# Attention block on one core: Yh's weights set over zeros so that the last product runs as 128x128 matmuls, four tiles of x, x loaded in quarters, small norms by one-tensor operations

## The reference, cut to what matters

```python
qkv = einsum('bcxy,oc->boxy', group_norm(x), w_qkv);  q, k, v = split(qkv)
k = softmax(k, axis=-1)
context = einsum('ndm,nem->nde', k, v)
content_out = einsum('nde,ndm->nem', context, q)
Sx = einsum('ndxy,xid->nixy', q4, Px)            # Px: relative row table
Yh = einsum('nixy,neiy->nexy', Sx, v4)
Yh = batch_norm(Yh)                               # one mean and variance per e, over all images and heads
Sy = einsum('ndxy,yid->nixy', q4, Py)            # Py: relative column table
rel_pos_out = einsum('nixy,nexi->nexy', Sy, Yh)
x + einsum('bcxy,oc->boxy', content_out + rel_pos_out, w_out) + b_out
```

## Time and profile before

| | |
|---|---|
| median of 3 runs | 3025.26 us (3024.06 to 3027.86) |
| the profiled execution | 3016.12 us, span 3014.0 us |
| mean granted clock of PE | 0.953 of full speed |
| busy: PE, PEld, DVE, ACT, POOL | 2656.9, 2127.2, 1875.2, 1544.1, 1248.7 us |
| matmuls | 61044 |
| bytes moved by the transfers | 383.62 MB, 127 GB/s on average |

### The profile page before, as it was taken

One profiled execution on the slowest core, in us unless ns is written; L12 is line 12 of the kernel. 1 busy time (PEld: TensorE's weight loads), 2 busy tenths in 40 slices (PEclk: granted clock), 3 DMA queues, 4 the chain that ended last, 5 costly groups with the idle time before them and its releaser, 6 DMA issues. The chain is left out here.

```text
span 3014.0 us, 131462 instructions
## 1 busy us (share of the span) xinstructions
PE 2656.9 (88%) x61044; PEld 2127.2 (71%) x61044; DVE 1875.2 (62%) x2986; ACT 1544.1 (51%) x2884; POOL 1248.7 (41%) x557
## 2 busy tenths in 40 slices
PE   2999999999998998999989986887979888888889
PEld 1788787787787877878778775666666666666665
DVE  5567667676676676676675556655555555555553
ACT  1565565655656656566565553444443444344443
POOL 2244334424325335244253336544444444454641
PEclk9999999999999999999999997899999999999999
DMA  3233434425325235234235337767666766666663
GB/s 143 60 85 115 100 74 128 102 59 149 81 66 162 61 77 153 60 90 139 70 98 121 95 94 159 176 173 173 176 171 174 173 173 171 168 175 182 178 179 106
DMA packets 433042, 383.62 MB, mean 127 GB/s; under 512 B 297840, under 2 KB 364656, under 8 KB 430448
## 3 DMA queue, kind: packets, MB, share of 16 engines
q1 hardware_dynamic: 414064, 341.66, 44.1%
q10 hardware_dynamic: 18432, 33.56, 3.1%
HBM read 206.31 MB, written 168.82 MB: 124 GB/s over the span
## 5 line engine op out<-in xcount | busy, mean ns | idle before, releaser
L787 POOL TENSOR_TENSOR k_f<-k_f,negmax 128x1024 f32<-128x1024 f32 x128 | 303.4, 2399 | 851.7 <-DVE negmax L752 851.7
L430 PE MATMUL bank<-w_hi,x_hi 128*128 128x256 f16 x2048 | 576.6, 282 | 39.0 <-POOL x_lo L771 23.4
L430 PE MATMUL bank<-w_lo,x_hi 128*128 128x256 f16 x2048 | 570.7, 279 | 2.5 <-issue 2.5
L430 PE MATMUL bank<-w_hi,x_lo 128*128 128x256 f16 x2048 | 569.9, 278 | 0.3 <-issue 0.3
L1241 POOL TENSOR_TENSOR x_f<-x_f,y_norm_by 128x1024 f32<-128x1024 f32 x127 | 273.3, 2152 | 552.5 <-DMA x_f<-y_scratch 550.2
L697 DVE TENSOR_TENSOR v_lo<-bank,v_hi 128x256 f16<-128x256 f32 x512 | 213.5, 420 | 261.7 <-ACT v_hi L565 260.6
L564 ACT ACTIVATE k_f<-bank 128x256 f32<-128x256 f32 x512 | 199.5, 390 | 315.3 <-PE bank L430 314.3
L1205 DVE TENSOR_TENSOR o_lo<-bank,o_hi 128x512 f16<-128x512 f32 x256 | 167.0, 684 | 279.6 <-ACT o_hi L1117 279.2
L1015 PE MATMUL bank<-q,rc_both 128*64 128x64 f16 x4096 | 276.2, 245 | 64.6 <-DMA q<-q_scratch 32.7
L1117 ACT ACTIVATE o_hi<-bank 128x512 f16<-128x512 f32 x256 | 142.1, 594 | 370.7 <-PE bank L1046 370.7
L430 PEld LDWEIGHTS bank<-w_hi,x_hi 128*128 128x128 f16 x2048 | 297.5, 145 | 47.4 <-issue 23.5
(11 more groups left out here) (146 smaller groups left out, 8293.3 us busy)
## 6 DMA issues: line engine op xcount, KB each, us to landing
y_scratch<-yst SPq DMA_DIRECT2D x256, 256.0 KB, 3.8
x_f<-y_scratch SPq DMA_DIRECT2D x256, 256.0 KB, 5.3
q<-q_scratch SPq DMA_DIRECT2D x256, 256.0 KB, 4.7
x_f<-x SPq DMA_DIRECT2D x16, 2048.0 KB, 11.3
q_scratch<-q_hi SPq DMA_DIRECT2D x128, 256.0 KB, 3.4
q_scratch<-q_lo SPq DMA_DIRECT2D x128, 256.0 KB, 4.1
x_res<-x SPq DMA_DIRECT2D x128, 256.0 KB, 6.9
out<-x_res ACTq DMA_DIRECT2D x128, 256.0 KB, 3.3
```

Source lines behind the costliest of these rows:

```text
L430: mm = pe.matmul(outs, lhs[a], rhs[m], start=first and n == 0, stop=last and n == 2, **kw)
L787: pool.tensor_tensor(kk, kk, negmax[:, :].unsqueeze(1).to_broadcast([P, 8, P]), ALU.add).then_inc(shifted, 1)
```

## The change

Half two, the product: `yb_hi` and `yb_lo` get one more dimension of 2 before the channel, [128, 32, 2, 64, 2]. Partitions 0 to 63 (the first head) fill index 0 and hold zeros at index 1; partitions 64 to 127 hold zeros at index 0. So the weights of one x and both heads are one 128x128 matrix with two 64x64 blocks and zeros elsewhere, and one 128x128 matmul of 64 columns takes the place of two 64x64 ones. The zeros are set once by four memsets on DVE. ACT and DVE fill the two blocks by one operation on 64 partitions each, in place of one on 128, and the semaphores count 8 pieces a head. Both content sets stand ahead of the products, and each bank of the pair signals when it is filled.

The tiles: twice the size of `yb` is made up for by `XS` = 4 slots of `x_res`, and by `st` and `y_norm_by`, which now lie in other tiles. The loads into the slots are moved: tiles 0 to 3 at the last two pairs of head 2, 4 to 11 at the second and fourth pair of head 3, 12 to 15 at the second pair of head 0.

The loads of q: by head of the pair and in halves of x. One (half, head) part is two transfers of the same bytes as before but twice the length of a piece (2 KB). They are issued after the second and third ro pair (one part each) and after the fourth (two parts).

Half one: the small operations of the two norms that read two tensors from SBUF become `tensor_scalar` with per-partition scalars, one for each channel block where needed. The next image is loaded in quarters of a channel block, with a semaphore for each block, spread over heads 0 and 1 of the turn.

```diff
-                for c in range(CC):
-                    sp.dma_start(x_f[:, c, :], x_chunks[0, c]).then_inc(x_in, 16)
+                def load_x(index, c, quarter):
+                    s = slice(quarter * XC, quarter * XC + XC)
+                    sp.dma_start(x_f[:, c, s], x_chunks[index, c][:, s]).then_inc(x_in[c], 16)
...
+                            if order is not final_turn and hp < CC and (hp, quarter) != (0, 0):
+                                load_x(b + 1, hp, quarter)
+                        next_x(0)
                         store_ys(0, 1)
                         if hp < HP - 1:
                             store_q(0)
+                        next_x(1)
                         store_ys(2, 3)
...
-                    dve.scalar_tensor_tensor(ymv[:, 1:2], ymv[:, 0:1], ymv[:, 0:1], ymv[:, 1:2],
-                                             ALU.mult, ALU.add).then_inc(y_stats, 1)
+                    dve.tensor_scalar(ymv[:, 1:2], ymv[:, 0:1], ymv[:, 0:1], ymv[:, 1:2],
+                                      ALU.mult, ALU.add).then_inc(y_stats, 1)
                     dve.wait_ge(y_stats, n + 3)
-                    dve.tensor_tensor(acc[:, :], acc[:, :], ymv[:, :], ALU.add).then_inc(y_stats, 1)
+                    for k in range(2):
+                        o = dve.tensor_scalar(acc[:, k:k + 1], acc[:, k:k + 1], ymv[:, k:k + 1], None, ALU.add)
+                    o.then_inc(y_stats, 1)
...
-                    dve.tensor_tensor(rstd[:, :], gs[:, :, 0], gs[:, :, 0], ALU.mult).then_inc(bn_done, 1)
-                    dve.wait_ge(bn_done, base + 2)
-                    dve.tensor_tensor(rstd[:, :], gs[:, :, 1], rstd[:, :], ALU.subtract).then_inc(bn_done, 1)
+                    for c in range(CC):
+                        dve.tensor_scalar(rstd[:, c:c + 1], gs[:, c, 0:1], gs[:, c, 0:1], gs[:, c, 1:2],
+                                          ALU.mult, ALU.subtract).then_inc(bn_done, 1)
...
-        XS = 8
+        XS = 4
...
-            yb_hi = sb("yb_hi", [P, H // YB, DK, YB], F16, p2)
-            yb_lo = sb("yb_lo", [P, H // YB, DK, YB], F16, p2)
+            yb_hi = sb("yb_hi", [P, H // YB, 2, DK, YB], F16, p2)
+            yb_lo = sb("yb_lo", [P, H // YB, 2, DK, YB], F16, p2)
...
                             if i % 2 == 1 and more:
-                                load_q(b, hp + 2, i // 2)
+                                if i in (3, 5):
+                                    load_q(b, hp + 2, 0, i // 2 - 1)
+                                if i == 7:
+                                    for h in range(2):
+                                        load_q(b, hp + 2, 1, h)
...
-                            if hp == HP - 2 and i % 2 == 1:
-                                for u in range(i - 1, i + 1):
+                            if hp == HP - 2 and i >= 5 and i % 2 == 1:
+                                for u in range(i - 5, i - 3):
                                     load_residual(b, 0, u)
-                            if hp == HP - 1 and i == RO - 1 and order is not final_turn2:
-                                for u in range(XS, XS + 4):
+                            if hp == HP - 1 and i in (3, 7):
+                                for u in range(i + 1, i + 5):
                                     load_residual(b, 0, u)
...
                             content(0, cb_both)
-                            relative(0)
                             content(1, cb_rest)
-                            relative(1)
+                            for j in range(16):
+                                xx = 8 * i + j
+                                for k, (a, m) in enumerate(TERMS):
+                                    mm = pe.matmul(bank[:, banks[j // 8], j % 8 * 64:j % 8 * 64 + 64],
+                                                   (yb_hi, yb_lo)[a][:, xx // YB, :, :, xx % YB].rearrange("p h e -> p (h e)"),
+                                                   (sy_hi, sy_lo)[m][:, hp % 2, xx, :], start=False,
+                                                   stop=(j % 8 == 7 and k == 2), skip_group_check=True)
+                                if j % 8 == 7:
+                                    mm.then_inc(filled, 1)
...
+                for tile in (yb_hi, yb_lo):
+                    dve.memset(tile[0:64, :, 1, :, :], 0.0).then_inc(init, 1)
+                    dve.memset(tile[64:128, :, 0, :, :], 0.0).then_inc(init, 1)
...
                 def split_piece(t, hp, c):
-                    dve.wait_ge(yb_hi_done, t * YC + (c + 1))
                     s = slice(c * XA, (c + 1) * XA)
-                    dve.tensor_tensor(yb_lo[:, s, :, :],
-                                      y_f[:, hp % 2, :, c * XY:(c + 1) * XY].rearrange("p e (a x) -> p a e x", x=YB),
-                                      yb_hi[:, s, :, :], ALU.subtract).then_inc(yb_lo_done, 1)
+                    for h in range(2):
+                        own = slice(h * 64, h * 64 + 64)
+                        dve.wait_ge(yb_hi_done, t * (2 * YC) + (2 * c + h + 1))
+                        dve.tensor_tensor(yb_lo[own, s, h, :, :],
+                                          y_f[own, hp % 2, :, c * XY:(c + 1) * XY].rearrange("p e (a x) -> p a e x", x=YB),
+                                          yb_hi[own, s, h, :, :], ALU.subtract).then_inc(yb_lo_done, 1)
```

More of the change, by code:

```diff
@@ L155, in attention_kernel @@
         group = sb("group", [P, P], F32, p1)
-        x_in = sem("x_in", p1)
+        x_in = [sem(f"x_in{c}", p1) for c in range(CC)]
         with ExitStack() as st, nc.Block() as block:
@@ L183, in _ @@
                 for c in range(CC):
-                    sp.dma_start(x_f[:, c, :], x_chunks[0, c]).then_inc(x_in, 16)
+                    for k in range(4):
+                        s = slice(k * (PIX // 4), (k + 1) * (PIX // 4))
+                        sp.dma_start(x_f[:, c, s], x_chunks[0, c][:, s]).then_inc(x_in[c], 16)
                 for g in range(2):
@@ L641, in gn_channels @@
                     for c in range(CC):
[L642 to L643 removed]
+                        dve.tensor_scalar(mv[:, c, 1:2], mv[:, c, 0:1], mv[:, c, 0:1], mv[:, c, 1:2],
+                                          ALU.mult, ALU.add).then_inc(bn_done, 1)
                 def gn_scale(nth):
@@ L660, in gn_bias @@
                     dve.wait_ge(gn_root, nth + 1)
-                    dve.tensor_tensor(nbias[:, :], gs[:, :, 0], rstd[:, :], ALU.mult).then_inc(bn_done, 1)
-                    dve.wait_ge(bn_done, base + 6)
-                    dve.tensor_scalar(nbias[:, :], nbias[:, :], -1.0, None, ALU.mult).then_inc(bn_done, 1)
+                    for c in range(CC):
+                        dve.tensor_scalar(nbias[:, c:c + 1], gs[:, c, 0:1], rstd[:, c:c + 1], -1.0,
+                                          ALU.mult, ALU.mult).then_inc(bn_done, 1)
                 def gn_apply(nth, k):
@@ L944, in _ @@
                     sp.sem_inc(out_st[s], 16)
-                for c in range(YC):
-                    load_q(0, 0, c)
+                for k in range(4):
+                    load_q(0, 0, k // 2, k % 2)
                 load_context(0, 0)
-                for c in range(YC):
-                    load_q(0, 1, c)
+                for k in range(4):
+                    load_q(0, 1, k // 2, k % 2)
                 sp.wait_ge(cb_lo_done, 1)
@@ L1020, in turn @@
                             if i == 0:
+                                if order is first_turn2 and hp == 0:
+                                    pe.wait_ge(init, 5)
                                 pe.wait_ge(cb_lo_done, t + 1)
@@ L1037, in content @@
                                                       start=(g == 0 and k == 0), stop=False, skip_group_check=True)
-                            def relative(swap):
-                                for j in range(8):
-                                    for k, (a, m) in enumerate(TERMS):
-                                        for h in (swap, 1 - swap):
-                                            own = slice(h * 64, h * 64 + 64)
-                                            xx = 8 * (i + (h ^ swap)) + j
-                                            mm = pe.matmul(bank[own, banks[h ^ swap], j * 64:j * 64 + 64],
-                                                           (yb_hi, yb_lo)[a][own, xx // YB, :, xx % YB],
-                                                           (sy_hi, sy_lo)[m][own, hp % 2, xx, :], start=False,
-                                                           stop=(swap == 1 and j == 7 and k == 2), skip_group_check=True)
-                                            if swap == 1 and j == 7 and k == 2:
-                                                mm.then_inc(filled, 1)
                             content(0, cb_both)
-                            relative(0)
                             content(1, cb_rest)
-                            relative(1)
+                            for j in range(16):
[7 more added lines that the diff above has]
```

(1 more changed line is left out.)

54 lines of the change are left out of this document (28 added, 26 removed).

## The result

| | before | after |
|---|---|---|
| median of the undisturbed runs | 3025.3 us | 2989.1 us (2984.35 to 2990.20) |
| ratio, 95% interval | | 0.9887 (0.9859 to 0.9915) |
| profiled execution | 3016.12 us, span 3014.0 | 2984.35 us, span 2982.6 |
| clock of PE | 0.953 | 0.949 |
| busy: PE, DVE, ACT | 2656.9, 1875.2, 1544.1 us | 2606.9, 2163.3, 1711.7 us |

One more run of each kernel was disturbed as a whole and is left out. The change gains 1.1%, and the forecast was 3.3%. Of the span's 31.4 us, half one with the start of half two costs 6.4 (first content matmul at 1849.4 instead of 1842.9 us), the 32 heads give 46.6 back, and the end, from the start of PE's last matmul on, is 12.4 us instead of 3.7. The 46.6 come from the long heads, 0 and 3: these are 46 us shorter in all. The sixteen short heads, 1 and 2, have not changed (451.6 us together before, 451.3 now).

What follows compares the result with a forecast made beforehand. Half two: PE bounds but isn't fed, instructions arriving late; half one: PE waits on DVE. Half two -75, ends +15, half one -38: -98 us from span 3014.0 to 2916, median 2927, rounded to 2925; range 2870 to 3050.

Steps and rivals of the forecast that it cites:

- The product: Half two's 128x128 matmuls start 31 ns apart; a pair costs 0.2 us less, -26 us over 128 pairs.
- Rival A: Half two's new weights load slowly at a step of 4 bytes; total 3058 us; chance 0.15.
- Fewer instructions: 64 matmuls a pair, not 112: half of 116 us unexplained PE waits (-1.8 a head), 40% of lost clock (-1.1) return.
- rival B: Half two's unexplained waits and low clock don't fall, or DVE, sharing time with POOL, becomes the bound; 3025 to 3035; chance 0.17.
- The split in two halves: Half two's doubled DVE rests: +5.8 us DVE work a head, costing +1 us in short heads, 0.5 in long ones.
- half case: Rival B holding by half in half two: 2975 us, within rival B's chance of 0.17.
- q: Four q transfers after half two's last pair, not two: Sy waits +1.4 us a short head, long heads pay nothing.
- Small norms: Half one's norm passes stop stalling and take 0.17 us, shortening PE's waits for DVE: -38 us, bounds 0 and -55.
- rival C: The new small norm passes stall like the old ones: -60 us in all, 2965; chance 0.08.
- Quarters of the next image: Loading the next image in quarters in half one costs nothing: 0, bounds -8 to +10.
- Four tiles: Four x tiles: +0.5 us a long head; last image's bias, store, load turns of 6.1 us make the end +12 us.
- Start of half two: Four memsets on DVE hide in its idle time, the doubled first splits don't: +3 us, bounds 0 and +10.

Runs made afterwards that it cites:

- a_nosplit: Changed kernel with the rests of Yh's second head left out on DVE (output lacks that part): ratio 0.9639 to the kernel before, 2916 us.
- a_nopool: Changed kernel without POOL's second operation of the normalising (Yh gets its factor, not its addend): ratio 0.9700 to the kernel before, 2932 us.
- best_newq: Changed kernel, only Yh's high parts over zeros, one rest pass, x loaded as before, norm passes over 128x1, the change's q order: 0.9648 of the kernel before.
- a_oldq: Changed kernel with q loaded as before, two transfers after each pair: ratio 0.9857 to the kernel before.
- best: Changed kernel, only Yh's high parts over zeros, one rest pass, q and x loaded as before, norm passes over 128x1: 0.9571 of the kernel before, 2893.4 us.
- best_tail: As best, but in the last image ACT issues a tile's store one item later instead of three: 0.9563 of the kernel before, 2890.5 us.
- b_xstart: Kernel before with x loaded in quarters in half one, all eight issued at the start of the turn: ratio 0.9981.

## Why the prediction was wrong, point by point

The sum was -98 us; -36 us were measured in the medians. By parts, from the ratios of the single runs: norms -19 (forecast -38), quarters of x +15 (0), second half without q -41 (-82), q +9 (+22). They add up to -36, but each is known to some 6 us, q's to less, so that the fit is partly luck.

Within half two the traces give the heads' 46.6 us by terms. Against the forecast they are: product -50 (forecast -26), waits without a cause -107 (-58), low clock nothing (-35), PE's waits for DVE +77 (the split and the four tiles, +32), waits for q +34 (+22). The forecast's -75 also had a further 11 us off the short heads, "since the waits are denser there". By heads: the long ones gave 46 (forecast 43), the short ones nothing (32).

*The product* was right in mechanism, and gave twice what was forecast. Period 31 ns forecast, 29 measured from the starts; loads 98 ns, under 110; a pair's 48 matmuls take 1.50 us. A pair without waits at the high clock takes 2.93 us before and 2.55 now (medians), 0.39 less and not 0.2, since the two content sets in a row have become shorter too; over 128 pairs that is the 50 us. Rival A is out.

*Fewer instructions* was right on the waits, and too cautious: of 116 us in half two with no cause shown, 9 stay, not 58. That they were instructions arriving late fits this, but no run shows it by itself. The clock, put at -1.1 us a head, failed: 0.93 before and 0.92 now, where the forecast asked for over 0.95. The waits for DVE and q that took the place of the others are gaps as well. In the mean of the eight images the clock went from 0.95 to 0.98 in head 0, which came down from 45.1 to 39.8 us (images 3 to 8), and from 0.98 to 0.93 in head 3. So of rival B's "nothing of the 116 us and the clock comes back" the first half is refuted and the second is so.

*The split in two halves* is the step that failed: "+1 us in short heads and 0.5 in long ones". It had the right count and the wrong duration. The mean of the earlier trace rows, 1450 ns, was measured while POOL was busy for 47% of the time and DVE for 55%. In the changed kernel more of the passes are lengthened, 136 of 256 instead of 46 of 128, and by more. The second pass of a quarter starts right behind the first: it takes 2.07 us in the mean, the first 1.76. So the mean came to 1915 ns: 305 us more instead of the 186. a_nosplit's single passes of the new form, 1787 ns, say that the doubling isn't all of it; what else lengthens the first pass isn't shown. The floor of a short head, put at 23.7, is so 25 to 29 us, and their answers above. What the product and the fewer instructions could give a short head, 2 to 6 us by a_nosplit against before, ended in waits for DVE and q: a_nosplit gives back 73 us, and a_nopool 57 with DVE's own work unchanged. In the forecast's terms the split was put at +24 us over the half, and PE's waits for DVE rose by 77. Rival B named this mechanism ("whose two-tensor passes share time with POOL"), at 0.17; its half case, 2975, is the nearest of the prices to 2989. That half case had half of the waits without a cause and half of the low clock stay; nearly none of the first stayed and all of the second, so its number is luck.

*q* was right in mechanism, +1.4 us a short head, 22 us. It shows in full where DVE isn't behind it (best_newq, +23 us), and under DVE's wait it was worth 9 or nothing (a_oldq). I added two waits of PE that are largely one and the same time.

*Small norms* failed by half. I read the 0.17 us of the earlier trace rows as a one-tensor pass that doesn't stall. POOL was in fact idle in those 0.17 us: it had ended its third operation at 425.96 and waited for this very chain. The row before, 423.70 to 425.99, is the stall. The prediction said "0.17 us with POOL busy", and that was false: in all eight images the one-tensor passes over 128x2 of the kernel before ran with POOL idle. I had not put POOL's timeline beside DVE's. The kernel before shows it:

```profile
418.95 7.01 POOL L787 TENSOR_TENSOR k_f<-k_f,negmax 128x1024 f32<-128x1024 f32 x3 [33.15 <-DVE negmax L752]
426.47 0.70 POOL L776 TENSOR_TENSOR rstd<-rstd,minus_half 128x2 f32<-128x2 f32 x1 [0.50 <-DVE rstd L656]
```

The rule that I set aside for this row was right: the Trainium skill, "VectorE: DVE Perf Modes", "Two Vector instructions with no wait between them", as far as the 128x2 passes go, and so was rival C (0.08) for `gn_scale`. Over 128x1 there is no stall, and all the passes so written bring the rest: best, best_tail and best_newq, whose half one is that of before but for these passes, reach their first content matmul at 1805.7, 1814.1 and 1816.7 us where before has 1842.9. That is 26 to 37 us in single profiles, near the 38 of the forecast, for an edit that the change only half made.

*Quarters of the next image* were put at 0 with bounds -8 to +10 and cost 15 us. By b_xstart it is their place that costs; through which wait no trace shows. I had costed SP's issue time alone.

*Four tiles.* The end came 8.7 us later, forecast 12. The turns of bias and load are there, 4.7 us apart and not 6.1, and with the stores issued earlier the long end is gone (best_tail). ACT's bias in the last tiles:

```profile
2968.54 0.72 ACT L1123 ACTIVATE x_res<-x_res,bias 128x512 f32<-128x512 f32 x1 [4.08 <-DMA x_res<-x]
2973.22 0.72 ACT L1123 ACTIVATE x_res<-x_res,bias 128x512 f32<-128x512 f32 x1 [3.95 <-DMA x_res<-x]
2977.99 0.72 ACT L1123 ACTIVATE x_res<-x_res,bias 128x512 f32<-128x512 f32 x1 [4.05 <-DMA x_res<-x]
```

*Start of half two*: forecast +3. From the start of the last matmul of Yh's product in half one to the first content matmul it is 36.7 us, 33.3 before: +3.4. The four memsets take 1.76 us each and start 2.25 apart, from 1824.46 on:

```profile
1824.46 1.76 DVE L1181 MEMSET yb_hi<- 64x2048 uint32 x1 [0.37 <-issue]
...
1833.00 1.02 DVE L1186 TENSOR_TENSOR cb_rest<-c_f,cb_both 64x128 f16<-64x128 f32 x1
```

The first context's rest was at 1829.26 before.

## What to carry to other kernels

When work is added to an engine that another one can hold up, don't multiply the mean duration of before: take it apart into minimum and wait, and count how many of the new passes will start while the other engine is at work: two passes in a row both can. A short row beside a long one is evidence only with the other engine's timeline next to it. Put a doubled layout only on the operand whose copies an idle engine can make: here the high part, by ACT, which took the gain from 1.1% to 2.6% and, with the three other edits, to 4.3%. And look at which stages a gain can reach: the long heads here could take it, the short ones had DVE close behind.

## What the runs showed that I had not expected

DVE passes over 128x2 float32 that read one tensor end with POOL's running operation (1.55 and 2.28 us instead of 0.17), and ones over 128x1 take 0.14 to 0.28 us in every image, with POOL busy beside them in seven of the eight. A two-tensor pass of 1.2 us takes up to 3.0. The Trainium skill, "SBUF — State Buffer", section "Who interferes with whom", tells of a pair of ports that DVE and GpSimd lock for a whole instruction while the other waits in full; a `tensor_scalar` from SBUF to SBUF takes it where its mode with two ports fits, for which "VectorE: DVE Perf Modes", section "Mode 2×_2P — use both read ports for one tensor", wants an outermost dimension (one of size 1 aside) that is even, or odd and the same on both sides. Ends within 0.05 us of POOL's, for two numbers and never for one, agree; no run has a pass over three.

POOL's own normalising pays too: its second operation, at 1933 ns in the median before, is at 2781 after.

```profile
L1265 POOL TENSOR_TENSOR x_f<-x_f,ones x127: 1921/2781/2815, 1826.2 to 2905.8; 128x1024 f32<-128x1024 f32 x127
```

Weights of 128 columns at a step of 4 bytes load in 98 ns, as quickly as contiguous ones, so what makes line 430's loads slow (144 ns) is the longer step alone or something beside it; no run here tells.
